# A gated cross-attention block with a top-8 router on one core: the router chain's scratch moved to PSUM, its gate and negations folded away, mask rows loaded for two units at once, and six transfers of the last unit issued from ScalarE

## What is computed

```
h   = layernorm(x, over the 2048 positions)
q,k = Wq h + bq, Wk h + bk        (256 channels, 8 heads of 32)
v   = Wv ctx + bv
att = softmax(q k / sqrt(32), masked) inside windows of 128 positions
x   = x + tanh(g0) * mask * (Wo gelu(att v) + bo)
h   = layernorm(x, over the 2048 positions)
s   = softmax(h Wr + rb)          (64 experts, one row per channel)
w   = the 8 largest of s, the rest 0
x   = x + tanh(g1) * (h * sum(w) + w eb)
```

## Time and profile before

| | us |
|---|---|
| median of three runs | 1213.76 |
| the profiled execution | 1211.18 |
| its span on the core | 1209.0 |
| PE busy, of the span | 1125.2 (93%) |
| DVE busy | 975.0 (81%) |
| ACT busy | 1028.9 (85%) |
| POOL busy | 707.7 (59%) |

### The profile page before, as it was taken

How to read it: one execution, slowest core, us unless ns; L and a number is a source line. 1 busy time by engine, 2 the same in 40 slices (tenths; PEclk the granted TensorE clock), 3 DMA queues, 4 the chain that set the end, 5 groups by cost and what they waited for, 6 DMA issues and landing times.

```text
span 1209.0 us, 33323 instructions
## 1 busy us (share of the span) xinstructions
PE 1125.2 (93%) x11661; PEld 1045.5 (86%) x11661; DVE 975.0 (81%) x1882; ACT 1028.9 (85%) x3200; POOL 707.7 (59%) x660
## 2 busy tenths in 40 slices
PE   3699999999999899999999999998999999999977
PEld 3698999889988899798997989988998889979955
DVE  6667878988789877989779977988779987797757
ACT  4688999889989899988998989898898889989944
POOL 2365777467655567557764666646764656655621
PEclk9899999999999999999999999999999999999989
DMA  9267554785548854596546865478444884555433
GB/s 289 75 175 198 139 131 116 232 214 149 132 116 249 222 130 126 147 261 181 128 127 216 217 165 129 115 244 226 117 126 123 259 218 120 130 161 178 104 85 139
DMA packets 169766, 199.82 MB, mean 165 GB/s; under 512 B 27776, under 2 KB 104704, under 8 KB 169472
## 3 DMA queue, kind: packets, MB, share of 16 engines
q1 hardware_dynamic: 168736, 197.69, 60.3%
q10 hardware_dynamic: 864, 0.01, 0.0%
HBM read 80.06 MB, written 33.65 MB: 94 GB/s over the span
## 4 chain that ended last, share of the span: by engine, by line
PE 53%; SPq 21%; DVE 9%; ACT 5%; issue 5%; DMA 4%; POOL 3%; DVEq 0%; ACTq 0%; POOLq 0%
SPq L520 14%; PE ring L309 7%; PE ring L311 6%; PE ring L310 6%; PE ring L365 4%; DVE X L888 3%; PE ring L348 3%; PE ring L324 3%; PE ring L326 3%; PE ring L325 3%; PE ring L384 3%; PE ring L385 3%; PE ring L386 3%; SPq L525 3%; PE ring L403 3%
## 5 line engine op out<-in xcount | busy, mean ns | idle before, releaser
L614 ACT ACTIVATE P<-ring,nmx 128x128 f32<-128x128 f32 x1024 | 358.6, 403 | 32.1 <-DVE nmx L754 31.8
L309 PE MATMUL ring<-z_hi,wqk_hi 128*128 128x256 f32 x1024 | 299.3, 292 | 22.9 <-DVE z_lo L953 21.0
L310 PE MATMUL ring<-z_hi,wqk_lo 128*128 128x256 f32 x1024 | 292.3, 285 | 0.0
L311 PE MATMUL ring<-z_lo,wqk_hi 128*128 128x256 f32 x1024 | 292.2, 285 | 0.0
L614 ACT ACTIVATION_READ_ACCUMULATOR P<-ring,nmx 128x1 f32 x1024 | 248.9, 243 | 0.0
L1046 POOL TENSOR_TENSOR z_lo<-z,z_hi 128x1024 fp32r<-128x1024 f32 x62 | 147.6, 2381 | 166.8 <-ACT z_hi L582 166.8
L309 PEld LDWEIGHTS ring<-z_hi,wqk_hi 128*128 128x128 f32 x1024 | 198.0, 193 | 35.4 <-DVE wqk_lo L928 20.9
L1058 POOL TENSOR_TENSOR X<-X,xt 128x512 f32<-128x512 f32 x128 | 165.5, 1293 | 68.3 <-DVE xt L789 68.2
L761 DVE STREAM_TRANSPOSE T<-P 128x512 f32<-128x512 f32 x256 | 169.1, 690 | 44.6 <-ACT P L614 28.2
L311 PEld LDWEIGHTS ring<-z_lo,wqk_hi 128*128 128x128 f32 x1024 | 198.7, 194 | 0.0
L310 PEld LDWEIGHTS ring<-z_hi,wqk_lo 128*128 128x128 f32 x1024 | 198.5, 194 | 0.0
(11 more groups left out here) (137 smaller groups left out, 2696.1 us busy)
## 6 DMA issues: line engine op xcount, KB each, us to landing
PT<-T SPq DMA_DIRECT2D x1024, 80.0 KB, 2.1
cx<-in_ctx SPq DMA_DIRECT2D x128, 256.0 KB, 3.7
out_y<-X SPq DMA_DIRECT2D x128, 256.0 KB, 3.1
X<-in_x SPq DMA_DIRECT2D x112, 256.0 KB, 4.7
mg<-in_mask SPq DMA_DIRECT2D x64, 128.0 KB, 3.3
X<-in_x SPq DMA_DIRECT2D x8, 512.0 KB, 7.5
sel<-rows_d SPq DMA_DIRECT2D x256, 3.0 KB
X<-in_eb SPq DMA_DIRECT2D x2, 512.0 KB, 8.2
```

Of the source, the lines that this page charges most:

```text
L309: e.matmul(o, wqk_hi[:, t, cols], z_hi[:, t, :], t == 0, False)
L310: e.matmul(o, wqk_lo[:, t, cols], z_hi[:, t, :], False, False)
L311: last = e.matmul(o, wqk_hi[:, t, cols], z_lo[:, t, :], False, t == DT - 1)
L614: last = e.activation(P[:, n, :], bank("S", 4 * u + g)[:, k * W:(k + 1) * W], ACT.Exp, bias=nmx[u % 2][:, n:n + 1], accum_out=den[u % 2][: ...
```

## The change

- **Scratch in PSUM.** The tile `lr` of the router chain goes; its 256 columns lie in the upper half of the bank LT (`low(b)`), and the weights are multiplied there and no longer in `ex`. The sum of the weights and the gain lie in LT's first columns. LT is therefore held until `c_scale` is done (`ac_v`) and no longer until `c_top` (`lg_v`).
- **Gate and negations.** `c_gate` goes. `c_scale` makes the gain by one operation of three inputs (sum times tanh(g1) times 1/std) and the offset by another (gain times -1 times mean). The negated means go: x is normalised by a subtraction.
- **Eps.** Variance plus eps is made on GpSimd, ahead of the power, with a semaphore between them.
- **Mask rows.** A `sel` tile now holds the rows of two units, loaded by four transfers, in two buffers, and the matmul of line 340 reads the two windows twice.
- **Last transfers.** The last unit's move issues 10 of its 16 transfers on SyncE's queue and 6 on ScalarE's (`move_rest`).

```diff
-    norm2=27.5, c_gate=33.5, L=36, LT=34, c_top=38.75, c_exp=37.75, c_w=40.75, c_sc=40.75, wT=43, wt_hi=43.25, wt_lo=42.25, mix=43.75, m_gap=0.25,
+    norm2=27.5, L=36, LT=34, c_top=38.75, c_exp=37.75, c_w=40.75, c_sc=40.75, wT=43, wt_hi=43.25, wt_lo=42.25, mix=43.75, m_gap=0.25,
...
-NRW = 3
+NRW = 2
...
-        mv = sb("mv", [128, DT, 2])
+        mv = [sb(f"mv{i}", [128, DT, 2]) for i in range(2)]
...
-        ln1 = [sb(f"ln1_{i}", [128, 3, DT]) for i in range(2)]
-        ln2 = sb("ln2", [128, 3, DT])
+        rs1 = [sb(f"rs1_{i}", [128, DT]) for i in range(2)]
+        rs2 = sb("rs2", [128, DT])
...
             for b in batch(t, C["LT"]):
-                take(("LT", b), t, C["c_top"] - C["LT"], lg_v, b + 1)
+                take(("LT", b), t, C["c_sc"] - C["LT"], ac_v, b + 1)
...
-                e.wait_ge(rows_in[u % NRW], 64 * (u // NRW + 1))
+                e.wait_ge(rows_in[u // 2 % NRW], 64 * (u // 2 // NRW + 1))
                 for g in range(4):
                     _, freed, n = bank_of["S", 4 * u + g]
                     if freed:
                         e.wait_ge(freed, n)
                     head = slice(32 * g, 32 * g + 32)
-                    e.matmul(bank("S", 4 * u + g)[:], ones3[head, :], sel[u % NRW][head, :, :].rearrange("p k i -> p (k i)"),
-                             True, False)
+                    e.matmul(bank("S", 4 * u + g)[:], ones3[head, :],
+                             sel[u // 2 % NRW][head, 2 * (u % 2):2 * (u % 2) + 2, :].rearrange("p w i -> p (w i)").unsqueeze(
+                                 1).to_broadcast([32, 2, U]), True, False)
...
-            def load_rows(u):
-                if u >= NRW:
-                    e.wait_ge(s_pe, u - NRW + 1)
-                elif u == 0:
+            def load_rows(n):
+                if n >= NRW:
+                    e.wait_ge(s_pe, 2 * (n - NRW + 1))
+                elif n == 0:
                     e.wait_ge(sm_rowsd, 16)
                     e.wait_ge(v_set, V_SEL)
                 for g in range(4):
-                    e.dma_start(sel[u % NRW][32 * g + 12:32 * g + 15, :, :].rearrange("k (m w) i -> k m (w i)", m=2),
-                                rows_d[:, 2 * u:2 * u + 2, :].rearrange("k w i -> k (w i)").unsqueeze(1).to_broadcast(
-                                    [3, 2, U])).then_inc(rows_in[u % NRW], 16)
+                    e.dma_start(sel[n % NRW][32 * g + 12:32 * g + 15, :, :], rows_d[:, 4 * n:4 * n + 4, :]).then_inc(
+                        rows_in[n % NRW], 16)
 
             def move(u):
                 e.wait_ge(tp_v, 4 * (u + 1))
                 e.wait_ge(td_v, u + 1)
                 if u:
                     e.wait_ge(on_v, u)
-                for b in range(4):
-                    for a in range(4):
-                        e.dma_start(PT[32 * b:32 * b + 32, a, :, :], T[u % 2][32 * a:32 * a + 32, b, :, :]).then_inc(pt_in, 16)
+                for n in range(16 if u < TU - 1 else LAST_SP):
+                    a, b = n % 4, n // 4
+                    e.dma_start(PT[32 * b:32 * b + 32, a, :, :], T[u % 2][32 * a:32 * a + 32, b, :, :]).then_inc(pt_in, 16)
...
+            def move_rest(u):
+                e.wait_ge(tp_v, 4 * (u + 1))
+                e.wait_ge(td_v, u + 1)
+                e.wait_ge(on_v, u)
+                for n in range(LAST_SP, 16):
+                    a, b = n % 4, n // 4
+                    e.dma_start(PT[32 * b:32 * b + 32, a, :, :], T[u % 2][32 * a:32 * a + 32, b, :, :]).then_inc(pt_in, 16)
...
             def norm2(b):
                 e.wait_ge(bn2_v, 16 * (b + 1))
+                if b:
+                    e.wait_ge(ac_v, b)
                 for t in range(DT):
                     e.bn_aggr(mv2[:, t, :], bn2[:, t, :, :].rearrange("p a c -> p (a c)")).then_inc(agg2_v, 1)
-                if b:
-                    e.wait_ge(ac_v, b)
-                e.wait_ge(agg2_v, DT * (b + 1))
-                e.tensor_scalar(ln2[:, 0, :], mv2[:, :, 0], -1.0, None, ALU.mult).then_inc(neg2_v, 1)
-                e.tensor_scalar(ln2[:, 1, :], mv2[:, :, 1], EPS, None, ALU.add).then_inc(neg2_v, 1)
 
             def r_low(u, a):
...
-            def c_gate(b):
+            def c_top(b):
                 if b == 0:
                     e.wait_ge(sm_rb, 16)
                     e.wait_ge(sm_small, 96)
-                e.wait_ge(neg2_v, 2 * b + 2)
-                e.wait_ge(rstd2_g, b + 1)
-                e.tensor_scalar(gate[:, 0, :], ln2[:, 2, :], cst[:, TF:TF + 1], None, ALU.mult).then_inc(dm_v, 1)
-                e.wait_ge(dm_v, b + 1)
-                e.tensor_tensor(gate[:, 1, :], gate[:, 0, :], ln2[:, 0, :], ALU.mult).then_inc(gate_v, 1)
-
-            def c_top(b):
                 e.wait_ge(rstd2_g, b + 1)
                 e.wait_ge(lt_pe, b + 1)
                 for t in range(DT):
                     last = e.scalar_tensor_tensor(out=lg[:, t, :], in0=bank("LT", b)[:, t * NX:(t + 1) * NX],
-                                                  scalar=ln2[:, 2, t:t + 1], in1=rbb[:], op0=ALU.mult, op1=ALU.add)
+                                                  scalar=rs2[:, t:t + 1], in1=rbb[:], op0=ALU.mult, op1=ALU.add)
...
-                    last = e.match_replace(lr[:, t, :], t8[:, t, :], lg[:, t, :], -3.0e38)
+                    last = e.match_replace(low(b)[:, t, :], t8[:, t, :], lg[:, t, :], -3.0e38)
                 last.then_inc(mr_v, 1)
                 e.wait_ge(mr_v, b + 1)
-                e.tensor_tensor(lr[:], lr[:], lg[:], ALU.not_equal).then_inc(sel_v, 1)
+                e.tensor_tensor(low(b), low(b), lg[:], ALU.not_equal).then_inc(sel_v, 1)
+
+            def low(b):
+                return bank("LT", b)[:, DT * NX:2 * DT * NX].rearrange("p (t x) -> p t x", t=DT)
 
             def c_weights(b):
                 e.wait_ge(ex_a, b + 1)
                 e.reciprocal(sc[:, :, 3:4], sc[:, :, 1:2]).then_inc(wm_v, 1)
                 e.wait_ge(sel_v, b + 1)
-                e.tensor_tensor(ex[:], ex[:], lr[:], ALU.mult).then_inc(wm_v, 1)
+                e.tensor_tensor(low(b), low(b), ex[:], ALU.mult).then_inc(wm_v, 1)
                 if b:
                     e.wait_ge(wT_pe, b)
                 e.wait_ge(wm_v, 4 * b + 2)
-                e.tensor_tensor(w2[:], ex[:].unsqueeze(2).to_broadcast([128, DT, 2, NX]),
+                e.tensor_tensor(w2[:], low(b).unsqueeze(2).to_broadcast([128, DT, 2, NX]),
                                 sc[:, :, 3:4].unsqueeze(3).to_broadcast([128, DT, 2, NX]), ALU.mult).then_inc(w2_v, 1)
 
             def c_scale(b):
                 e.wait_ge(w2_v, b + 1)
-                e.tensor_reduce(sc[:, :, 5:6], w2[:, :, 0, :], AX.X, ALU.add).then_inc(wm_v, 1)
-                e.wait_ge(gate_v, b + 1)
+                wsum, gain = bank("LT", b)[:, 0:DT], bank("LT", b)[:, DT:2 * DT]
+                e.tensor_reduce(wsum, w2[:, :, 0, :], AX.X, ALU.add).then_inc(wm_v, 1)
                 e.wait_ge(wm_v, 4 * b + 3)
-                e.tensor_tensor(sc[:, :, 4:5], sc[:, :, 5:6], gate[:, 0, :].unsqueeze(2), ALU.mult).then_inc(wm_v, 1)
-                e.tensor_tensor(sc[:, :, 7:8], sc[:, :, 5:6], gate[:, 1, :].unsqueeze(2), ALU.mult)
+                e.scalar_tensor_tensor(out=gain, in0=wsum, scalar=cst[:, TF:TF + 1], in1=rs2[:], op0=ALU.mult,
+                                       op1=ALU.mult).then_inc(wm_v, 1)
                 e.wait_ge(wm_v, 4 * b + 4)
-                e.tensor_scalar(sc[:, :, 6:7], sc[:, :, 4:5], 1.0, None, ALU.add).then_inc(ac_v, 1)
+                e.scalar_tensor_tensor(out=sc[:, :, 7], in0=gain, scalar=-1.0, in1=mv2[:, :, 0], op0=ALU.mult, op1=ALU.mult)
+                e.tensor_scalar(sc[:, :, 6], gain, 1.0, None, ALU.add).then_inc(ac_v, 1)
...
                 e.wait_ge(bn1_v, 16 * (b + 1) - 4)
-                if b:
-                    e.wait_ge(rstd1_g, b)
                 if b >= 2:
                     e.wait_ge(z32_g, NU * (b - 1) + 1)
                 for t in range(DT):
                     if b or t != TA:
-                        e.bn_aggr(mv[:, t, :], bnst[:, t, :, :].rearrange("p a c -> p (a c)")).then_inc(agg1_v, 1)
-                if b == 0:
-                    e.wait_ge(st_a, 6)
-                e.wait_ge(agg1_v, DT * (b + 1) - 1)
-                e.tensor_scalar(ln[:, 0, :], mv[:, :, 0], -1.0, None, ALU.mult).then_inc(neg1_v, 1)
-                e.tensor_scalar(ln[:, 1, :], mv[:, :, 1], EPS, None, ALU.add).then_inc(neg1_v, 1)
+                        e.bn_aggr(mv[b % 2][:, t, :], bnst[:, t, :, :].rearrange("p a c -> p (a c)")).then_inc(agg1_v, 1)
...
             def norm2(b):
-                e.wait_ge(neg2_v, 2 * (b + 1))
-                e.tensor_tensor(ln2[:, 2, :], ln2[:, 1, :], half[:], ALU.pow).then_inc(rstd2_g, 1)
+                e.wait_ge(agg2_v, DT * (b + 1))
+                e.tensor_scalar(rs2[:], mv2[:, :, 1], EPS, None, ALU.add).then_inc(eps2_g, 1)
+                e.wait_ge(eps2_g, b + 1)
+                e.tensor_tensor(rs2[:], rs2[:], half[:], ALU.pow).then_inc(rstd2_g, 1)
 
```

(9 more changed lines are left out.)

37 lines of the change are left out of this document (17 added, 20 removed).

## The result

The changed kernel takes **1231.14 us** (median of 4 runs, 1229.50 to 1234.01). The kernel before, on the same chip, takes 1211.89 (1205.31 to 1215.45, 4 runs). The ratio is 1.0163, 95% interval 1.0131 to 1.0194: **slower by 1.6%**, where I had forecast faster by 1.2% and given any loss a chance of 0.03. The profiled execution has a span of 1228.7 us for 1209.0, at a granted clock of 0.985.

The account below looks back on a forecast made before the run. PE's own work was taken to bound plain units, with savings where PE waits: boundaries 10.5, mask rows 1.5, tail 2.4, together 14.4 us off 1213.76, so 1199.4 us; range 1191 to 1207.5.

Parts of the forecast that it names:

- Gate and negations: At a batch boundary VectorE's gate costs 2.1 us; without it the logits come 0.9 to 1.0 us earlier.
- the bank's wait: Rival: PE's output projection waits for `c_scale` to free bank LT, making the kernel slower; chance 0.03.
- SyncE's tie to cx_lo: Behind a boundary SyncE's context load must wait for cx_lo, so SyncE can gain only 0.4 us there.
- Plain units: Units of 15.92 us, set by PE's own work; nothing that the change takes from VectorE can shorten them.
- The boundary: Between batches PE's first mix and first add come earlier: 1.5 us at each of seven, 10.5 us; bounds 4 to 15.
- the PSUM rival: PSUM operands cost time and hold-ups move to another operation: 0.6 us remain per boundary, 1206.4 us; chance 0.14.
- From boundary to end: The 1.5 us saved at each of seven boundaries counted whole in the kernel's time, 10.5 us.
- Mask rows: SyncE's queue behind the stores: 0.25 us for six batches, 1.5 us saved; bounds 0 and 10.
- Last transfers: Tail: the last unit's line 365 starts at 1169.6 for 1172.00, 2.4 us saved; bounds 0 and 3.2.
- Eps: Moved to GpSimd, which waits there anyway: no effect on the time; at the start 0, bounds -0.2 and +0.3.
- four signs: Profile after: waits ahead of first mix 0.6 us, PV starts 26.1 apart, `c_scale` 1.1 to 1.2, PT<-T waits down 4.
- three signs that I had named for being wrong: PE's projection waits for VectorE's factor; small operations still show 1.2 us; waits for PT<-T fall below 10.

Follow-up runs that it names:

- the mended kernel: The changed kernel with GpSimd's normalisation adding a negated mean again, made by GpSimd once per batch: 1198.82 us (ratio 0.9915), and 1200.89 (0.9917) when run again.

## Why the prediction was wrong

- **The step that failed** is the change part by part, "Gate and negations". It counts what leaves VectorE with the negated means and says nothing of the instruction that used them. GpSimd's 252 normalisations were the same in number, shape and place, so I carried them at their old 561 ns and never gave the exchange of `add` for `subtract` a term or a bound. It measured 1236 ns. No row of the kernel before has this form with a subtraction, so the price could not be read there; that it was unread could have been said, with a chance for it. Of 170 us of added GpSimd time 30 to 32 reached the end, because GpSimd had idle time, but in a fixed order, ahead of cx_lo, on which SyncE's queue hangs.
- **The rivals** had none for it either. The slower one was the bank's wait; it didn't happen. The projection started 1.0 us behind the end of `c_scale`, with a wait for ot_lo of 0.16. No rival looked at the two engines that the change left "as they were", though SyncE's tie to cx_lo stood in my own working.
- **Plain units**: "nothing that the change takes from VectorE can shorten it" was true, and the wrong question. They could be lengthened.
- **The boundary** was right in sum, in part by luck, since its two terms were each off: 1.5 us forecast, 1.5 measured, 26.1 us between the PV starts forecast and measured; waits 0.39 for a forecast 0.6; `c_scale` 0.88 for 1.1 to 1.2. Its parts were the other way round: the gate 1.0 forecast, 0.4 measured (in the kernel with scratch in SBUF the comparison takes 1072 ns on the mean for 671 before, so the hold-up moved on to it, which the PSUM rival had as its condition), the scratch 0 forecast and 1.1 measured. My reading of the gate's hold-up by two SBUF inputs also left out line 827, which has one input tensor and was held up too. The PSUM forms do cost a little, 247 ns for 204 for the replacement, as bounded.
- **From boundary to end** the sum was wrong: I let 7 x 1.5 us arrive whole. 4 to 5 arrived. What is late next was SyncE's transfers behind the boundary, whose waits I had in the earlier trace rows and treated as a term apart. Without the subtraction's price this is the largest error of the sum, some 6 us.
- **Mask rows**: 1.5 forecast; 7.6 in the profile where they come without the chain (with the split), 2.7 by the medians in the mended kernel, there within the noise. The step that failed is the tie to cx_lo: the load at 681.71 had 6.2 us of slack and not 0.4, and the queue issued without a pause two units beyond the stores. The sum behind the boundaries is where both this part and the chain's act, so the two parts don't add.
- **Last transfers**: 2.4 forecast, 1.4 measured; PE's own list was the bound as named, but it ran at the lower clock for longer, and that is the missing 1.0 us. The objection that I drew from the Trainium skill (DMA: Bandwidth & Descriptors, "Issuing engines are not separate DMA queues") would have left 0 if the transfers were the bound. The page lets only the time of issuing be saved. In the trace that is what was saved, and the issue's 0.63 us was the bound: the sixteen were through 7.4 us behind the first issue, where SyncE alone takes 10.00 to issue them and line 365 started 11.5 behind it.
- **Eps** cost nothing visible: 232 ns and a power 20 ns longer, ahead of the same wait.
- **What would show it**: of four signs, the two waits and the boundary came as written, `c_scale` came a little shorter than written, and the fourth, PE's waits for the transfers, rose to 31.7 us for a forecast fall to 16. That pointed at SyncE's queue. None of the three signs that I had named for being wrong appeared; the loss came on a way that none of them watched.

Without the subtraction the forecast of 14.4 us was still too high: the mended kernel gains 10 us (0.0084 of 1210), 6 to 14 over the intervals of its two measurements. That its median of 1199 to 1201 meets the forecast time of 1199.4 is luck: the kernel before ran at 1210 beside it and not at 1213.76, and the parts came to 10 us and not to 14.4.

## What to carry to other kernels

When an edit replaces an operation by an "equal" one (a sign moved, an add for a subtract), it is a new instruction until a row shows its price on that engine; ask it of every engine that uses the tile, not only of the one the edit is meant for. Where GpSimd must subtract a per-partition number, negate it once and add. A microsecond saved ahead of a stretch that already waits for transfers is worth less than a microsecond: read what is late next, and count the parts that share that slack once. When a wait looks like a tie, count which completion it waits for before you trust the tie. In this kernel, taking one held-up operation out moved the hold-up to the next one with two SBUF inputs; giving that one an input in PSUM ended it.
